# Expert results added by an accumulating scatter, a later place for the late plan, and the shift on GpSimd

## The reference

```
x  = layernorm(x + attention_layer(x))        # 16 heads of 64, causal, own FFN of 512, gelu
g  = softmax(x @ gate_w + gate_b)             # 8 experts; the best two, weights scaled to sum 1
y  = sum over the two experts e of  weight_e * (relu(x @ w1[e] + b1[e]) @ w2[e] + b2[e])
out = layernorm(x + y)                        # over the 128 values of each token
```

## Time and profile before

| | us |
|---|---|
| median of three runs | 681.49 |
| lowest and highest | 680.2, 681.53 |
| the profiled execution | 683.78 |
| its span, first to last instruction | 681.8 |
| TensorE busy | 653.0 |
| VectorE busy | 529.3 |
| ScalarE busy | 441.2 |
| GpSimd busy | 248.4 |

### The profile page before, as it was taken

The page is one execution under the profiler, slowest core; times in us unless marked ns, Lnnn a source line. Parts: engine busy times, 40 slices in busy tenths (PEclk is TensorE's granted clock), DMA queues, the critical chain, the costliest instruction groups (busy, mean ns, idle before and its releaser), DMA issues.

```text
span 681.8 us, 23205 instructions
## 1 busy us (share of the span) xinstructions
PE 653.0 (96%) x9322; PEld 558.5 (82%) x9322; DVE 529.3 (78%) x1565; ACT 441.2 (65%) x879; POOL 248.4 (36%) x273
## 2 busy tenths in 40 slices
PE   5899999999999999999999999999989989999995
PEld 4678878888888888788878888887769989999983
DVE  5877788887898788888878887888877777666675
ACT  5665785578568666946784786568447555666646
POOL 6400014035114312431341233034216557666664
PEclk9999999999999999999999999999989999999998
DMA  8430010011101000100110010001131233254536
GB/s 245 129 72 3 2 33 18 18 34 33 33 14 54 17 18 19 49 26 15 30 47 17 20 33 2 18 20 32 30 92 41 68 110 118 82 155 129 170 133 185
DMA packets 46953, 40.27 MB, mean 59 GB/s; under 512 B 9152, under 2 KB 41536, under 8 KB 46848
## 3 DMA queue, kind: packets, MB, share of 16 engines
q1 hardware_dynamic: 37264, 25.78, 13.4%
q0 software_dynamic: 4784, 10.39, 4.5%
q10 hardware_dynamic: 4800, 2.62, 1.4%
HBM read 23.12 MB, written 15.66 MB: 57 GB/s over the span
## 4 chain that ended last, share of the span: by engine, by line
PE 67%; DVE 17%; ACT 11%; issue 2%; DMA 0%; POOL 0%; DVEq 0%; ACTq 0%; POOLq 0%
PE banks_o L764 9%; PE banks_sc L592 5%; PE banks_o L572 5%; PE banks_o L584 4%; DVE work L1308 4%; PE bank_u L605 3%; PE bank_q L457 3%; PE bank_q L459 3%; PE bank_u L565 3%; PE bank_q L458 3%; ACT work L947 2%; DVE work L1324 2%; PE bank_k L457 2%; PE banks_sc L457 2%; PE banks_sc L469 2%
## 5 line engine op out<-in xcount | busy, mean ns | idle before, releaser
L1776 POOL DMA_INDIRECT routed_rows<-routed,slot x64 | 63.1, 986 | 140.1 <-DVE slot L1304 89.7
L870 ACT ACTIVATE work<-bank_u 128x384 f32<-128x384 f32 x64 | 31.4, 491 | 76.0 <-PE bank_u L605 75.8
L1324 DVE TENSOR_TENSOR work<-banks_sc,causal 128x1024 f32<-128x1024 f32 x64 | 77.7, 1214 | 0.0
L764 PE MATMUL banks_o<-w,work 128*128 x624 | 77.6, 279 | 0.0
L764 PEld LDWEIGHTS banks_o<-w,work 128*128 128x128 f32 x624 | 74.3, 195 | 0.3 <-issue 0.2
L572 PE MATMUL banks_o<-v_aug,work 128*64 128x65 f32 x2048 | 70.7, 221 | 0.0
L572 PEld LDWEIGHTS banks_o<-v_aug,work 128*64 128x64 f32 x2048 | 65.3, 138 | 0.0
L1308 DVE SCALAR_TENSOR_TENSOR work<-bank_k,work 128x512 f32<-128x512 f32 x64 | 44.1, 689 | 21.2 <-ACT work L947 21.2
L1308 DVE SCALAR_TENSOR_TENSOR work<-bank_q,work 128x512 f32<-128x512 f32 x64 | 43.7, 683 | 19.9 <-ACT work L941 19.6
L592 PE MATMUL banks_sc<-work 64*64 64x128 f32 (+1 forms) x2048 | 55.8, 247 | 0.2
L1766 POOL TENSOR_TENSOR gT_lo<-work,gT_hi 128x512 fp32r<-128x512 f32 x28 | 37.2, 1348 | 50.4 <-DVE gT_hi L1238 50.4
(11 more groups left out here) (338 smaller groups left out, 1828.7 us busy)
## 6 DMA issues: line engine op xcount, KB each, us to landing
work<-in_L_attn_x SPq DMA_DIRECT2D x16, 256.0 KB, 2.9
work<-routed_rows SPq DMA_DIRECT2D x20, 132.0 KB, 2.1
xg_more<-routed_rows SPq DMA_DIRECT2D x19, 132.0 KB, 2.1
stage<-in_L_ffn_w SPq DMA_DIRECT2D x8, 256.0 KB, 2.6
moe_input<-routed SPq DMA_DIRECT2D x8, 256.0 KB, 2.7
work<-moe_input ACTq DMA_DIRECT2D x8, 256.0 KB
v_aug<-expert_results SPq DMA_DIRECT2D x4, 512.0 KB, 6.2
out<-work SPq DMA_DIRECT2D x6, 256.0 KB, 2.8
```

The costliest lines, as they stand in the source:

```text
L764: mm = pe.matmul(Y[t % 2][:, blk(k)], hTe[t % 2][:, f, blk(k)], w2[:, bass.ds(e[t] * F + f * D, D)], start=(f == 0), stop=(f == NF - 1))
L1324: dve.tensor_tensor(am_all.rearrange("p (x m) s -> p x (m s)", m=2), sc_banks.rearrange("p (x s) -> p x s", s=2 * P), causal[:, :, :].rear ...
L1776: pool.indirect_dma_start(rows_d, bass.IndirectOffsetOnAxis(slot[:, k, c:c + 1], 0), routed[:, c, k, :], None).then_inc(sct, 16)
```

## The change

x3 is no longer kept apart. SP stores it into the even rows of `expert_results` and zeros into the odd ones, sequence by sequence, and the expert results are scattered with addition onto them (`compute_op=ALU.add`). A unit is then the sum of two rows: one addition on VectorE (units 0 to 2) or two terms on TensorE (units 3 to 9). The loads of x3 go. In the late plan, VectorE and ScalarE get a new order for tiles 9 to 11: biases and row copies move ahead of the plan's parts, and the three late parts stand one tile later. SP loads tile 16 in the middle of the padding stores. The shift is computed by GpSimd behind its power (`unit_scale`), from a negated mean that VectorE writes; unit 0's goes ahead of the last two tiles' scatters. Semaphores and constants that follow from this are left out below.

```diff
-BY_PE = list(range(2, 10))
+BY_PE = list(range(3, 10))
...
-    x3_d = nc.dram_tensor("moe_input", (TOKENS, D), F32, kind="Internal").ap()
+        zeros = sb("zeros", [P, D])
...
+        def result_rows(b, k):
+            return res_d[2 * b * T:2 * (b + 1) * T, :].rearrange("(c p k) d -> p c k d", p=P, k=2)[:, :, k, :]
...
SyncE:
+                sp.dma_start(result_rows(b, 1), zeros[:, :].unsqueeze(1).broadcast_to([P, CH, D])).then_inc(zero_st, 16)
                 if b + 2 < E:
                     sp.wait_ge(w1lo, b + 1)
...
-                sp.dma_start(by_chunk(x3_d[b * T:(b + 1) * T, :]), routed[:, :, 0, 0:D]).then_inc(x3_st, 16)
+                sp.dma_start(result_rows(b, 0), routed[:, :, 0, 0:D]).then_inc(x3_st, 16)
             load_x(xres, 0, ld_xres)
+            sp.wait_ge(cst, CST_ALL)
...
-            load_tile(EARLY - 1)
+                if e == E // 2 - 1:
+                    load_tile(EARLY - 1)
...
TensorE (unit_sum):
                 pe.matmul(out, ident[:, :], unit_pairs(u, 0), start=True, stop=False)
-                pe.matmul(out, ident[:, :], unit_pairs(u, 1), start=False, stop=False)
-                pe.matmul(out, ident[:, :], unit_rows(u), start=False, stop=True).then_inc(c_mm, 1)
+                pe.matmul(out, ident[:, :], unit_pairs(u, 1), start=False, stop=True).then_inc(c_mm, 1)
...
-            pe.wait_ge(ld_x3, 16 * B)
...
ScalarE:
-            def load_x3(i):
-                act.dma_start(xc[:, i, :, :], x3_d[i * T:(i + 1) * T, :].rearrange("(c p) d -> p c d", p=P)
-                              ).then_inc(ld_x3, 16)
...
-            weigh(7)
             rows_hi(10)
             w1_stage(10)
+            weigh(7)
             hidden_relu(9)
+            rows_hi(11)
+            w1_stage(11)
             weigh(8)
-            late = {EARLY + 2 + i: lambda i=i: load_x3(i) for i in range(B)}
-            for t in range(9, TILES):
+            hidden_relu(10)
+            weigh(9)
+            for t in range(10, TILES):
...
-                if t == EARLY + 1:
-                    act.wait_ge(x3_st, 16 * B)
-                    act.wait_ge(pad_st, 16 * E)
-                if t in late:
-                    late[t]()
+            act.wait_ge(pad_st, 16 * E)
...
VectorE:
-            def unit_first(u):
+            def unit_add(u):
                 dve.wait_ge(ld_z[u], 16)
-                dve.tensor_tensor(unit_rows(u), unit_rows(u), unit_pairs(u, 0), ALU.add).then_inc(z_sum, 1)
-
-            def unit_second(u, nth):
-                dve.wait_ge(z_sum, nth)
-                dve.tensor_tensor(unit_rows(u), unit_rows(u), unit_pairs(u, 1), ALU.add).then_inc(c_sb, 1)
-                dve.wait_ge(c_sb, nth)
+                dve.tensor_tensor(unit_rows(u), unit_pairs(u, 0), unit_pairs(u, 1), ALU.add).then_inc(c_sb, 1)
...
+                dve.tensor_scalar(u_nm[:, u, 0:n], u_mv[:, u, 0:n, 0], -1.0, None, ALU.mult)
                 dve.tensor_scalar(u_ve[:, u, 0:n], u_mv[:, u, 0:n, 1], EPS_LN, 1.0, ALU.add, ALU.mult).then_inc(c_ve, 1)
-
-            def unit_shift(u):
...
             top2(b)
+            rows_lo(10)
             bias2(7)
-            rows_lo(10)
+            place(b, R)
             w1_stage(10)
             hidden_relu(9)
-            place(b, R)
+            rows_lo(11)
+            bias2(8)
             plan_classes()
+            w1_stage(11)
+            hidden_relu(10)
             fill_padding()
             plan_padding()
-            bias2(8)
-            late = {9: plan_counts, 10: lambda: experts_of(le2, REST, ntc2[:, :], step2[:, :]),
-                    11: lambda: rows_of(le2, EARLY, REST), 34: lambda: unit_first(0), 35: lambda: unit_second(0, 1),
-                    36: lambda: unit_stats(0), 37: lambda: unit_first(1), 38: lambda: unit_second(1, 2)}
-            for t in range(9, TILES):
+            bias2(9)
+            late = {10: plan_counts, 11: lambda: experts_of(le2, REST, ntc2[:, :], step2[:, :]),
+                    12: lambda: rows_of(le2, EARLY, REST), 34: lambda: unit_add(0), 35: lambda: unit_add(1),
+                    36: lambda: unit_stats(0), 37: lambda: unit_add(2)}
+            for t in range(10, TILES):
...
GpSimd:
+            then(pool.memset(zeros[:, :], 0.0), False)
...
                 apart(pool)
+                if t == 0:
+                    pool.wait_ge(zero_st, 16 * B)
+                    pool.wait_ge(x3_st, 16 * (B - 2))
+                if t == EARLY:
+                    pool.wait_ge(x3_st, 16 * B)
                 pool.wait_ge(yw_sb, t + 1)
                 for k in range(2):
                     pool.indirect_dma_start(res_d, bass.IndirectOffsetOnAxis(xg[n][:, k, D:D + 1].bitcast(U32), 0),
-                                            yw[t % YRING][:, k, :], None).then_inc(res_st[n], 16)
+                                            yw[t % YRING][:, k, :], None, compute_op=ALU.add).then_inc(res_st[n], 16)
...
-            def unit_rstd(u):
+            def unit_scale(u):
...
                 pool.tensor_tensor(u_rs[:, u, 0:n], u_ve[:, u, 0:n], neg_half[:, 0:n], ALU.pow).then_inc(c_r, 1)
+                pool.wait_ge(c_r, nth)
+                pool.tensor_tensor(u_nmr[:, u, 0:n], u_nm[:, u, 0:n], u_rs[:, u, 0:n], ALU.mult).then_inc(c_nm, 1)
...
-            for t in range(9, TILES):
+            for t in range(9, TILES - 2):
                 store(t)
-            for u in TURN:
-                unit_rstd(u)
+            unit_scale(0)
+            store(TILES - 2)
+            store(TILES - 1)
+            for u in TURN[1:]:
+                unit_scale(u)
```

More of the change, by code:

```diff
@@ L176, in build @@
         u_stats, u_mv = per_chunk(6), per_chunk(2)
-        u_ve, u_rs, u_nmr = (per_chunk(1)[:, :, :, 0] for _ in range(3))
+        u_ve, u_rs, u_nmr, u_nm = (per_chunk(1)[:, :, :, 0] for _ in range(4))
         assert spot[0] <= WORK * T
@@ L276, in build @@
             sem(n) for n in ("xt_mm", "l1_mm", "l2_mm", "xt_hi", "xt_lo", "w1_now_hi", "w1_now_lo", "ht_a", "ht_v", "yb_sb", "yw_sb"))
-        ld_x3 = sem("ld_x3")
+        zero_st = sem("zero_st")
         ld_z = [sem(f"ld_z{u}") for u in range(len(UNITS))]
-        z_sum, c_sb, c_mm, c_st, c_mv, c_ve, c_r, c_nm, c_out = (
-            sem(n) for n in ("z_sum", "c_sb", "c_mm", "c_st", "c_mv", "c_ve", "c_r", "c_nm", "c_out"))
+        c_sb, c_mm, c_st, c_mv, c_ve, c_r, c_nm, c_out = (
+            sem(n) for n in ("c_sb", "c_mm", "c_st", "c_mv", "c_ve", "c_r", "c_nm", "c_out"))
         out_st = sem("out_st")
@@ L287, in by_chunk @@
             return rows.rearrange("(c p) d -> p c d", p=P)
-        CST_ALL = 16
+        def result_rows(b, k):
+            return res_d[2 * b * T:2 * (b + 1) * T, :].rearrange("(c p k) d -> p c k d", p=P, k=2)[:, :, k, :]
+        CST_ALL = 17
         PLAN_ROWS = 13
@@ L320, in unit_bank @@
         def unit_bank(u):
-            bk = (bkB, bkY, bkF, bkC, bkE, bkA, bkH, bkG)[BY_PE.index(u)]
+            bk = (bkB, bkY, bkF, bkE, bkA, bkH, bkG)[BY_PE.index(u)]
             n = UNITS[u][2]
@@ L1612, in unit_stats @@
                     dve.wait_ge(c_mm, BY_PE.index(u) + 1)
+                else:
+                    dve.wait_ge(c_sb, u + 1)
                 for c in range(n):
@@ L1621, in unit_stats @@
                 dve.wait_ge(c_mv, nth)
+                dve.tensor_scalar(u_nm[:, u, 0:n], u_mv[:, u, 0:n, 0], -1.0, None, ALU.mult)
                 dve.tensor_scalar(u_ve[:, u, 0:n], u_mv[:, u, 0:n, 1], EPS_LN, 1.0, ALU.add, ALU.mult).then_inc(c_ve, 1)
-            def unit_shift(u):
-                n = UNITS[u][2]
-                dve.wait_ge(c_r, TURN.index(u) + 1)
-                dve.scalar_tensor_tensor(out=u_nmr[:, u, 0:n], in0=u_mv[:, u, 0:n, 0], scalar=-1.0, in1=u_rs[:, u, 0:n],
-                                         op0=ALU.mult, op1=ALU.mult).then_inc(c_nm, 1)
             g_last = B * PAIRS - 1
@@ L1684, in _ @@
             top2(b)
+            rows_lo(10)
             bias2(7)
-            rows_lo(10)
+            place(b, R)
             w1_stage(10)
             hidden_relu(9)
-            place(b, R)
+            rows_lo(11)
+            bias2(8)
             plan_classes()
+            w1_stage(11)
+            hidden_relu(10)
             fill_padding()
             plan_padding()
-            bias2(8)
-            late = {9: plan_counts, 10: lambda: experts_of(le2, REST, ntc2[:, :], step2[:, :]),
-                    11: lambda: rows_of(le2, EARLY, REST), 34: lambda: unit_first(0), 35: lambda: unit_second(0, 1),
-                    36: lambda: unit_stats(0), 37: lambda: unit_first(1), 38: lambda: unit_second(1, 2)}
-            for t in range(9, TILES):
+            bias2(9)
[3 more added lines that the diff above has]
+            for t in range(10, TILES):
                 if t == 34:
-                    dve.wait_ge(ld_x3, 16 * B)
+                    dve.wait_ge(pad_st, 16 * E)
                 if t + 2 == EARLY:
@@ L1709, in _ @@
                     late[t]()
-            unit_stats(1)
-            unit_stats(2)
```

(19 more changed lines are left out.)

## The result

Six executions of each kernel: before 681.13 us (680.2 to 682.51), after **705.89 us** (703.97 to 707.73), a ratio of 1.036 [1.0341, 1.038]. The forecast was 676.6 with a range to 682.0. The profiled execution of after took 706.28 us with a span of 704.5, that of before 683.78 and 681.8.

What follows compares the result with a forecast made beforehand. TensorE, busy 96% of the span, was taken as the bound. Late plan 3.7 and end 1.2 us off the profiled 683.78 gave 678.9; on the median of 681.49, 2.3 lower, 676.6 us, range 674.0 to 682.0.

Steps and rivals of the forecast that it cites:

- The scatter's duration: GpSimd's adding scatter instruction: 1.02 us, between 0.95 and 1.92, taken from a plain padding transfer of 1.18 us.
- c: The us one scatter instruction takes on GpSimd; a tile takes 2(c + 0.3) there.
- rival 1: GpSimd becomes the bound in the tile stage, passing 3.39 us a tile at c = 1.4; 713 us at 1.92; chance 0.14.
- slower than before from c = 1.39 on: Rival 1's break-even: 60 x 1.69 us from 564.7 is 666.1, the 4.9 us of the sum later.
- Landing: An adding scatter's writes land 3.3 us from issue, between 2.4 and 4.5; not felt in the stage.
- A slack of 3.7 us: Tile 17's load, behind tile 9's second scatter, is there by 571.7; TensorE wants it at 575.4; slack grows 0.8 a tile.
- The late plan: Tiles 8 to 14: the new VectorE and ScalarE order removes TensorE's hole, gaining 3.7 us, between 2.4 and 4.5.
- The end: Last units' sums and applications: GpSimd, ScalarE and loads all end near 677 instead of 678.24, gaining 1.2 us (+2.5 to -1.4).
- Presets: Eight zero stores of 256 KB in SP's queue and x3 to every second row cost nothing, hidden by TensorE's full stage.

Runs made afterwards that it cites:

- a1_order: The kernel before with only the new order of the late plan: 679.51 us, 0.9974 of before.
- e2_norm_first: The changed kernel with the last sequence's third layer-norm power moved ahead of tile 4's scatters: 704.15 us beside before at 682.24, 1.0331.
- e1_half: The changed kernel with the first of each tile's two scatters plain, only the second adding: 686.95 us beside before at 682.24, 1.007.
- a2_plain: The changed kernel with the addition taken out of the scatter and nothing else (results lack x3): 679.75 us, 0.9974 of before.
- b2_sizes: The changed kernel with four scatter forms in turn by tile (64 rows adding or plain, 128 adding at 256 or 512 B): one execution, 714.52 us, not compared.
- a3_add: The kernel before with only the adding scatter, onto rows preset with zeros by 16 stores: 706.08 us, 1.0363 of before.

## Why the prediction was wrong, step by step

**The scatter's duration: the step that failed.** I bounded c by 0.95 and 1.92 and took 1.02 from the plain transfer of the earlier trace rows, since "pieces are cheap". That row speaks of pieces, not of addition; it could not bear on a price that is paid once an instruction. Measured: 1.55 at 128 rows, 1.44 at 64. The range had to come from the bounds, whose middle, 1.44, lay already past the threshold of 1.4 that rival 1 names. 0.14 for it was far too little for a size that no row shows.

**Rival 1 was right in mechanism; its threshold was too high.** By its formula 60 x 1.85 us from 564.7 end at 676.0 instead of 661.3, +14.7 us. The rest of the trace's 706.28 follows on the profiled base of 678.9: +14.7 for the pitch, +8.1 for the start of tile 9's scatters (572.80, not 564.7), +2.6 between them and the last (unit 0's power and product, longer scatters), +2.2 behind the last scatter, -0.2 outside the span: 706.3. Of the 8.1, 2.5 are an error that has nothing to do with the addition: in a1_order tile 9's first scatter starts at 567.22. I had moved GpSimd forward by the 3.7 us that TensorE wins at tile 14, but its unbroken queue ahead of tile 9 begins with tile 7's scatters at 551.80, 0.8 earlier than before. 5.6 are the addition in the tiles ahead: 3.1 at tile 7's first scatter (554.86 against 551.80; the late power above), 2.5 for four scatters from there on. With the power moved (e2_norm_first) tile 7's first scatter starts at 552.00, so nearly all of the 3.1 is that power.

The same fixed start is why "slower than before from c = 1.39 on" does not hold: e1_half, with a mean c of 1.28, is already 0.7% slower. An estimate from three traces: between e1_half and after the last scatter's start moves by 18.6 us for 0.27 us of c, so the 6.9 us that e1_half lies behind a2_plain are gone at a c of about 1.2.

**Landing: right.** 3.3 forecast, median 3.4 measured. The Trainium skill (Collectives: The Full Stack, "The bandwidth ceiling: the fold count and why AG ≠ RS ≠ AR") has a reducing transfer read two sources for each write. The trace agrees in direction but not in size, for the landing came 1.0 us later (the instruction itself is 0.6 longer) where the prediction worked out 0.2 by the rule. The queue of scatters took 4.5% of the 16 engines before and 10.3% now, and each adding scatter has 112 more packets ((13520 - 4784) / 78).

```profile
q0 software_dynamic: 13520, 10.39, 10.3%
```

It isn't what costs the time: b2_sizes halves the bytes and the instruction stays at 1.6 us.

**"A slack of 3.7 us" for the load of tile 17: it held for plain scatters, not for adding ones** (in a2_plain TensorE works 5.00 of 5 us from 575 on). In after, tile 9's second scatter starts at 574.72, its load goes out at about 578.5, and TensorE stands 3.65 us until 580.87. The slack was priced with the same guess as the term itself, so it gave no protection when that failed.

**The late plan: right as a mechanism, half as much in the median.** After needs 22.3 us from tile 8 to 14 (553.01 to 575.28; forecast 22.5, before 26.2), and no clock under 0.9 shows there. But the gain in the median is 1.8 us. I had subtracted 3.7 from the profiled execution and then moved the result by the 2.3 us between this and the median, as if the two were independent: part of the 2.3 was probably low clock of the kind that the 3.7 removed.

**The end: 1.2 us forecast, none measured.** From the last scatter's end to the last application after needs 13.4 us (forecast 11.9, before 14.3), and from there to the end 4.3 us instead of the 3.6 put in. That TensorE's fewer terms are no gain by themselves was right, but the price of its idleness was left out. It stands 12.72 us for the last loads, and from 691 to 694 its granted clock is 0.50. GpSimd waits for the statistics behind it. TensorE and GpSimd in after, and the same unit's first term in before:

```profile
692.39 1.06 PE L783 MATMUL banks_sc<-gT_lo,ident 128*128 128x256 f32 x2
...
694.75 0.70 POOL L1869 TENSOR_TENSOR work<-work,neg_half 128x2 f32<-128x2 f32 x1 [1.69 <-DVE work L1619]
```

```profile
669.29 0.60 PE L776 MATMUL banks_sc<-gT_lo,ident 128*128 128x256 f32 x2
```

The unit's two terms take 2.1 us at that clock (691.38 to 693.45); its three terms took 1.5 before (669.29 to 670.74), and the forecast had 0.9.

**Presets: nothing, as said.** In a3_add 16 zero stores stand in SP's queue and the loss is that of after.

## What to carry to other kernels

When the term that decides has no row in the trace, find the value at which the sum changes sign and weigh the chances by where that lies between the bounds; the nearest row by look is not a measurement. A queue with 25% idle holds no 60% longer instructions: compute the pitch of every engine per tile (duration plus the 0.30 us between) before moving work onto it or making its work dearer, and ask how late its queue starts: e1_half was bound by GpSimd at a pitch of 3.16 us under TensorE's 3.39. And when a change removes a disturbance that the profiled execution shows, subtract it from that execution only, and ask whether the median has it.

## What the runs showed of the hardware

- An indirect DMA of GpSimd with addition takes 1.55 us of the engine for 128 rows and 1.44 for 64, against 0.96 and 0.92 without. 256 B rows cost 1.6. Its writes land at 3.4 us instead of 2.4.
- On two of the four chips of the experiments before takes 706 to 707 us instead of 681 to 682, with pauses put down to "issue" on TensorE and ScalarE; most of TensorE's lie between 569 and 584 us in all eight traces from them.
- TensorE standing for 2.85 us was followed by a stretch at a granted clock of 0.70, which is 0.6 of the stretch at the lower level (1.2 GHz); a pause of 3.65 us at 577 was followed by 0.91 between 580 and 600. After 12.72 us without a matmul the clock was 0.50, the lower level, from 691 to 694.
